# One-hots of a pair of windows written by one ScalarE instruction and moved by two SBUF DMAs

## What is computed

```python
y = affine(conv1x1(x, fc1_w, fc1_b), fc1_s, fc1_t)
nodes = windows of y, (1024, 64, 96)
idx = top_k(-dist, 9)           # nine nearest nodes of the same window
feat = concat(x_i, x_j - x_i)   # for each node i and neighbour j
h = max over j of gelu((feat @ ew + eb) * es + et)
x = affine(conv1x1(h, fc2_w, fc2_b), fc2_s, fc2_t) + x
```

## Time and profile before

| | |
|---|---|
| median of 3 runs | 4106.08 us (4105.18 to 4107.37) |
| the profiled execution's own time | 4102.94 us |
| its span | 4101.1 us |
| mean granted TensorE clock | 0.987 |
| TensorE, VectorE, ScalarE busy | 3901.0, 3821.5, 3694.2 us |
| GpSimd busy | 931.2 us |
| DMA moved | 272.31 MB, mean 66 GB/s |

### The profile page before, as it was taken

How to read it: one execution, slowest core, us unless ns; L and a number is a source line. 1 busy time by engine, 2 the same in 40 slices (tenths; PEclk the granted TensorE clock), 3 DMA queues, 4 the chain that set the end, 5 groups by cost and what they waited for, 6 DMA issues and landing times.

```text
span 4101.1 us, 79112 instructions
## 1 busy us (share of the span) xinstructions
PE 3901.0 (95%) x22752; PEld 2049.0 (50%) x22752; DVE 3821.5 (93%) x5162; ACT 3694.2 (90%) x6805; POOL 931.2 (23%) x1060
## 2 busy tenths in 40 slices
PE   4999999999999999999999999999999999999984
PEld 2445555455554555555555455555555455555542
DVE  2599999999999999999999999999999999999996
ACT  3899999999998999989999899989999899999983
POOL 0122222122222122222122222122222122222113
PEclk9999999999999999999999999999999999999996
DMA  1133342333333333343333333333333333433333
GB/s 50 24 64 76 58 88 51 67 76 66 73 73 66 60 75 73 58 80 57 69 75 66 73 61 75 62 69 76 62 79 57 70 66 67 81 61 59 62 66 65
DMA packets 100114, 272.31 MB, mean 66 GB/s; under 512 B 14946, under 2 KB 23394, under 8 KB 93476
## 3 DMA queue, kind: packets, MB, share of 16 engines
q0 software_dynamic: 65536, 184.58, 26.4%
q1 hardware_dynamic: 34116, 82.27, 7.5%
HBM read 77.68 MB, written 25.69 MB: 25 GB/s over the span
## 4 chain that ended last, share of the span: by engine, by line
PE 68%; DVE 11%; issue 9%; ACT 9%; DMA 1%; SPq 0%; POOL 0%; DVEq 0%; ACTq 0%; POOLq 0%
PE pg L648 18%; PE pmisc L576 9%; PE pg L651 8%; PE pvu L635 8%; DVE acc L1032 7%; PE pmisc L562 7%; PE pmisc L519 3%; PE pmisc L512 2%; PE pvu L621 2%; ACT MV L807 2%; PE pmisc L578 2%; DVE hid L1010 2%; PE pmisc L542 2%; PE pmisc L547 2%; ACT tapped L844 1%
## 5 line engine op out<-in xcount | busy, mean ns | idle before, releaser
L1032 DVE SCALAR_TENSOR_TENSOR acc<-hpad,w,acc 128x1024 f32<-128x1024 f32 (+1 forms) x2304 | 2618.2, 1160 | 33.5 <-issue 16.3
L648 PE MATMUL pg<-MV,VU 128*128 128x512 f32 x2048 | 1149.2, 643 | 40.7 <-ACT VU L815 29.8
L824 ACT ACTIVATE g<-pg 128x512 f32<-128x512 f32 x1536 | 912.5, 594 | 127.9 <-PE pg L651 81.4
L1010 DVE TENSOR_REDUCE hid<-g 128x192 f32<-128x1536 f32 x512 | 892.6, 1743 | 0.0
L429 POOL DMA_DIRECT2D acc<-tapped x256 | 241.3, 943 | 2106.8 <-DVE acc L1032 1818.8
L807 ACT ACTIVATE MV<-pvu,cst 64x512 f32<-64x512 f32 x1024 | 696.0, 680 | 11.8 <-PE pvu L621 5.0
L576 PE MATMUL pmisc<-acc,w 128*96 128x256 f32 x2048 | 497.1, 386 | 49.0 <-ACT acc L854 34.1
L651 PE MATMUL pg<-MV,VU 128*64 128x512 f32 x2048 | 527.5, 592 | 0.0
L562 PE MATMUL pmisc<-x,w 96*128 96x512 f32 (+1 forms) x1024 | 518.3, 608 | 7.0 <-ACT hpad L766 7.0
L635 PE MATMUL pvu<-wVU,y 97*64 97x192 f32 x4096 | 446.7, 339 | 21.8 <-ACT MV L807 21.2
L576 PEld LDWEIGHTS pmisc<-acc,w 128*96 128x96 f32 x2048 | 331.5, 165 | 262.6 <-issue 154.9
(11 more groups left out here) (101 smaller groups left out, 4447.6 us busy)
## 6 DMA issues: line engine op xcount, KB each, us to landing
acc<-tapped POOLq DMA_DIRECT2D x256, 512.0 KB, 4.9
xin<-in_x_dram SPq DMA_DIRECT2D x32, 768.0 KB, 5.8
invb<-rows_dram SPq DMA_DIRECT2D x32, 768.0 KB
x<-in_x_dram POOLq DMA_DIRECT2D x128, 192.0 KB, 4.4
res<-x POOLq DMA_DIRECT2D x128, 192.0 KB, 5.0
out_dram<-res SPq DMA_DIRECT2D x128, 192.0 KB, 3.2
hpad<-hpad SPq DMA_DIRECT2D x112, 33.0 KB, 1.8
g<-in_consts_dram SPq DMA_DIRECT2D x1, 640.0 KB
```

The costliest lines, as they stand in the source:

```text
L648: last = nc.tensor.matmul(ps[:, :], VU[:, r, part, 0:ONE128], cols[part], start=True, stop=True)
L824: nc.scalar.activation(g[:, p % 2, part, :, :], pg[(3 * p + part) % 2][:, :].rearrange("p (n k) -> p n k", k=KN), ACT.Gelu).then_inc(gelu_ ...
L1010: nc.vector.tensor_reduce(hid[:, c % 2, j, :, :], g[:, r], op=ALU.max, axis=AX.X).then_inc(hid_ready, 1)
L1032: nc.vector.scalar_tensor_tensor(out=dst, in0=src, scalar=wk, in1=dst, op0=ALU.mult, op1=ALU.add).then_inc(tap_done, 1)
```

## The change

`onehot` becomes one activation of 128 partitions into a new tile `onehots` ([128, 512] of f32, one buffer). SyncE then issues two DMAs of 64 partitions (128 KB each) that put the halves in their two places in `MV`. TensorE's `values` still waits for `onehot_ready`, now one activation; `gather` part 0 waits for a new semaphore `onehot_moved` (16 for each DMA). ScalarE's next `onehot` waits for `onehot_moved` of the pair before. The two DMAs stand at the start of SyncE's slot, ahead of its other transfers; the halo copy `UPPER_AT` moves from slot 2 to 3, the stores by one slot, the `invb` rows to the next slot. The identities in `MV` stay as they were. `hpad` loses eight unused rows, which makes room in SBUF.

```diff
-UPPER_AT, LOWER_AT = {2: FULL}, {5: FULL}
+UPPER_AT, LOWER_AT = {3: FULL}, {5: FULL}
...
-STORE_AT = {o + 2: q for o, q in W2_AT.items() if q % 2 == 1}
+STORE_AT = {o + 3: q for o, q in W2_AT.items() if q % 2 == 1}
...
+        onehots = sb("onehots", [128, KN * NODES])
...
-        hpad = sb("hpad", [128, 5, STRIP + 2, PADW])
+        hpad = sb("hpad", [128, FULL * (STRIP + 2) + STRIP // 2 + 2, PADW])
...
+            def move_onehots(P, p):
+
+                if due(count := 3 * P - 3):
+                    sp.wait_ge(gather_ready, count)
+                sp.sem_inc(sp_passed, 1)
+                if due(count := P + 1):
+                    sp.wait_ge(onehot_ready, count)
+                sp.sem_inc(sp_passed, 1)
+                for w in range(2):
+                    h = 64 * w
+                    sp.dma_start(MV[h:h + 64, p % 2, w, :], onehots[h:h + 64, :]).then_inc(onehot_moved, 16)
+
             def image(b, p0, p1):
                 for p in range(p0, p1):
+                    P = PAIRS * b + p
                     h = 1 if p < 16 else 0
                     if p % 16 == ROWS_AT and valid(b if h else b + 1, B):
-                        broadcast_norms(b, p, b if h else b + 1, h)
+                        store_norms(b, p, b if h else b + 1, h)
+                    if p % 16 == ROWS_AT + 1 and valid(b if h else b + 1, B):
+                        broadcast_norms(b if h else b + 1, h)
+                    if valid(P + 1, NPAIRS):
+                        move_onehots(P + 1, p + 1)
...
-                        if due(count := P + 1):
-                            pe.wait_ge(onehot_ready, count)
+                        if due(count := 32 * (P + 1)):
+                            pe.wait_ge(onehot_moved, count)
...
-                if due(count := 3 * P - 3):
-                    act.wait_ge(gather_ready, count)
-                for w in range(2):
-                    h = 64 * w
-                    last = nc.scalar.activation(MV[h:h + 64, p % 2, w, :].rearrange("p (n k) -> p n k", k=KN),
-                                                pone[h:h + 64, :, :].rearrange("p k n -> p n k"), ACT.Relu,
-                                                bias=nbias[h:h + 64, :], scale=1.0)
-                last.then_inc(onehot_ready, 1)
+                if due(count := 32 * P):
+                    act.wait_ge(onehot_moved, count)
+                nc.scalar.activation(onehots[:, :].rearrange("p (n k) -> p n k", k=KN), pone.rearrange("p k n -> p n k"),
+                                     ACT.Relu, bias=nbias, scale=1.0).then_inc(onehot_ready, 1)
```

More of the change, by code:

```diff
@@ L188, in sums_of, with rows_of @@
     return slice(g * STRIP * W + start, g * STRIP * W + start + n)
+def rows_of(g, first, end):
+    return slice((STRIP + 2) * g + first, (STRIP + 2) * g + end)
 def due(count):
@@ L300, in build @@
             "featT_ready", "featT_evac", "onehot_in", "onehot_ready"))
+        onehot_moved = sem("onehot_moved")
         vu_ready, vu_evac, gather_ready, gelu_done, chunk_ready = (sem(n) for n in (
@@ L338, in _, with store_norms @@
             load_half(0, 1)
-            def broadcast_norms(b, p, bi, h):
-                n = 2 * bi + h
+            def store_norms(b, p, bi, h):
                 fb, fp = when(b, p, ROWS_AT - 8)
@@ L346, in broadcast_norms @@
                 sp.dma_start(rows_dram.rearrange("k (r n) -> (k r) n", n=128), norm_rows[:, :]).then_inc(rows_stored, 16)
+            def broadcast_norms(bi, h):
+                n = 2 * bi + h
                 sp.wait_ge(rows_stored, 16 * (n + 1))
@@ L754, in shared_evac @@
                         h = 128 if gr < FULL else HALF
-                        nc.scalar.activation(hpad[0:h, gr, 1, 1:W + 1], ps[0:h, 0:W], ACT.Relu, bias=sh[0:h, :],
+                        nc.scalar.activation(hpad[0:h, (STRIP + 2) * gr + 1, 1:W + 1], ps[0:h, 0:W], ACT.Relu, bias=sh[0:h, :],
                                              scale=sc[0:h, :]).then_inc(misc_evac, 1)
@@ L764, in shared_evac @@
                         if m == 1 and t == STRIPS - 1:
-                            nc.scalar.activation(hpad[:, gr, STRIP + 1, 1:W + 1], zrow[:, :], ACT.Copy)
-                        nc.scalar.activation(hpad[:, gr, r0:r1, 1:W + 1],
+                            nc.scalar.activation(hpad[:, (STRIP + 2) * gr + STRIP + 1, 1:W + 1], zrow[:, :], ACT.Copy)
+                        nc.scalar.activation(hpad[:, rows_of(gr, r0, r1), 1:W + 1],
                                              ps[:, 0:(r1 - r0) * W].rearrange("p (row col) -> p row col", col=W),
@@ L770, in shared_evac @@
                         act.wait_ge(kept_half, 32 * s + 16)
-                        nc.scalar.activation(hpad[64:128, gr, 9, 1:W + 1], zrow[64:128, :], ACT.Copy)
+                        nc.scalar.activation(hpad[64:128, (STRIP + 2) * gr + 9, 1:W + 1], zrow[64:128, :], ACT.Copy)
                         for h, n in ((0, 8), (64, 7)):
                             last = nc.scalar.activation(
-                                hpad[h:h + 64, gr, 2:2 + n, 1:W + 1],
+                                hpad[h:h + 64, rows_of(gr, 2, 2 + n), 1:W + 1],
                                 ps[h:h + 64, 0:n * W].rearrange("p (row col) -> p row col", col=W),
@@ L837, in tap0 @@
                 nc.scalar.activation(acc[:, t % 2, sums_of(gr, 0, rows * W)].rearrange("p (row col) -> p row col", col=W),
-                                     hpad[:, gr, 0:rows, 0:W], ACT.Copy, scale=wd[:, gr, 0:1]).then_inc(tap0_done, 1)
+                                     hpad[:, rows_of(gr, 0, rows), 0:W], ACT.Copy, scale=wd[:, gr, 0:1]).then_inc(tap0_done, 1)
             def tap_product(b, p, s, gr):
@@ L926, in _ @@
             dve.sem_inc(consts_ready, 1)
-            nc.vector.memset(hpad[:, :, :, 0:1], 0.0)
-            nc.vector.memset(hpad[:, :, :, W + 1:PADW], 0.0)
+            nc.vector.memset(hpad[:, :, 0:1], 0.0)
+            nc.vector.memset(hpad[:, :, W + 1:PADW], 0.0)
             nc.vector.memset(zrow[:, :], 0.0)
@@ L1041, in image @@
                     bi = b if h else b + 1
-                    last = min(len(taps) - 1, 4) if p % PPC == 0 else 4
+                    last = max(3, min(len(taps) - 1, 4)) if p % PPC == 0 else 4
                     for a in taps[0:2]:
```

14 lines of the change are left out of this document (7 added, 7 removed).

## The result

The changed kernel took **4723.01 us** (median of 4 runs, 4714.77 to 4730.24) where the kernel before took 4106.43 in the same comparison (4105.18 to 4107.37). The ratio is 1.1502, with a 95% interval of 1.1488 to 1.1515: 617 us slower. The forecast, 4299, had the sign right and the size wrong by a factor of three, and the range ended at 4410. The profiled execution took 4720.71 us with a span of 4718.8.

What follows compares the result with a forecast made beforehand. TensorE, busy 95% of the span and holding the chain for 68%, was taken as the bound. Terms -38 + 0 + 160 + 37 + 34 = +193 us on the median 4106.1 gave 4299 us, range 4080 to 4410.

Steps and rivals of the forecast that it cites:

- ScalarE's relief, -38 us: One activation replaces two on ScalarE; 69 of TensorE's 133 waits for one-hots shorten by 0.55 us each: -38 us.
- Quiet slots, 0 us: Without GpSimd's transfers, the last half lands 2.5 us after the one-hots, inside every cover before the next gather: 0 us.
- The landing in the burst, +160 us: Slots 1, 9, 17, 25, beside GpSimd's four DMAs: landing 5.2 us against 2.73 of cover, 2.5 us on 64 slots: +160 us.
- Slots 14 and 30, +37 us: Beside one 512 KB GpSimd transfer, landing 4.1 us against 2.94 of cover, 1.2 us 32 times: +37 us.
- Behind SyncE's large transfers, +34 us: After slots 1, 9 and 25, the next one-hots queue behind 768 KB and a store: 0.7 us on 48 slots, +34 us.
- Moves cost nothing: Moving `UPPER_AT`, the stores and `invb` by a slot costs nothing, their readers being two slots or more away.
- A: Rival: transfers hidden, landing within 2.7 us also in slot 1, ScalarE's relief remains: about 4045 us; chance 0.16.
- B: Rival: partly late, landing in 3 to 4 us in busy slots, near even: about 4100 us; chance 0.13.
- D: Rival: the new activation costs as much as the two, so covers are 0.68 us shorter: 4400 us; chance 0.03.
- C: Rival: a queue that doesn't drain, the next slot also 2 us or more late: +400 us, 4500; chance 0.08.
- What would show it: Expected profile signs: ScalarE down some 350 us, gather part 0 waiting 2 to 3 us in busy slots, others unchanged.

Runs made afterwards that it cites:

- e5: Changed kernel, but one-hots of slots 1, 2, 5 and 6 of eight written straight into `MV`, the others by DMA: 4074.86 us, ratio 0.9934 to before.
- e7: Changed kernel with all one-hots written straight into `MV`, none by DMA; only the moved table rows and smaller `hpad` remain: 4080.13 us, ratio 0.9943 to before.
- E3: Changed kernel, but window 1's one-hots written straight and only window 0's sent, by one DMA of 64 partitions: 4539.93 us.
- e10: Changed kernel, but one DMA of 128 partitions takes both halves to window 0's place; window 1's gather reads a fixed table: 4625.43 us.
- e1: Changed kernel plus 22 unused matmuls ahead of gather part 0 in the slots that follow slot 1 of eight: 4457.83 us.
- e4: Changed kernel, but one-hots of slots 1, 5 and 6 of eight written straight into `MV`, the others by DMA: 4098.49 us, ratio 0.9984 to before.
- e9: Kernel before the change, with only the input half loads moved from slots 1 and 8 to 3 and 10: 4082.09 us, ratio 0.9948.
- e8: Changed kernel, but window 1's half is issued by ScalarE on its own queue: 4813.52 us.
- e6: Changed kernel, but only slots 3 and 7 of eight send one-hots by DMA, the others write them straight: 4076.32 us, ratio 0.9936 to before.
- e11: e5 with the input halves loaded in slots 3 and 10: 4077.11 us, ratio 0.9927 to before.

## Why the prediction missed

**ScalarE's relief, -38 us.** The instruction was right (0.685 us for 0.68; the one-hots' own busy time fell from 696.0 to 350.6 us, ScalarE's in all by 315 for 348). What it is worth was too high: e5 and e7 differ by 5 us. The prediction put 64 of the 133 waits in slots 1, 9, 17 and 25; the trace of before has 48 there (48.2 us), 33 in slots 3 of eight (24.3) and 29 in slots 0 (15.4). In e5 the waits of slots 0 and 3 are gone but for 5 (4.6 us), and only slot 3 is shorter, by 11 us in all: in slot 0 the landing took more than the relief gave, and part of slot 3's went the same way (31 of e5's 57 gather waits are behind slot 3, 12.4 us). A freed wait is worth what no other wait takes over.

**Quiet slots, 0 us.** The landing was right, the term wasn't quite. The second half landed 2.93 us after the one-hots, near the upper bound of 3.0: each DMA takes 2.2 to 2.3 us, and the second is issued 0.51 us behind the first, not 0.37. Slots 4, 8 and 24 kept their length. Slots 0 and 16 didn't: away from the turns both took 7.17 us and now 7.74 and 7.62. The cover there is 2.60 us, in slot 0 too, where the prediction read 3.1 or more and named slot 16 alone. That is 12 us over the 25 such slots that aren't at a turn, and it doesn't show in the table because the turns got shorter by more. E3 and e10, which land inside 2.60 us, have 7.17 in slot 16.

**The landing in the burst, +160 us.** The step "I stay under that: 5.2 us" failed. It measured 6.8 us, and the slot grew by 4.08, not 2.5: **261 us**. The working had 5.6 to 7.5 from packets and took a value below it, on the argument that the first GpSimd transfer has only just begun. The trace shows no such head start: the first packet starts 2.05 us after the issue, in a quiet slot 1.12, and then 128 packets take 3.75 us, in a quiet slot 1.32. The Trainium skill ("DMA: Bandwidth & Descriptors", Queues, rings and completion order) says that an engine drains a whole packet of descriptors of one queue before it turns to the next. The estimate of near 7 us and 270 us, which the prediction worked out from it and set aside, came out; whether by its mechanism isn't shown, since the trace doesn't tell which DMA engine moved a packet. This step was short by 101 us. By itself it would have left the forecast at 4400, still inside the range; what took the result out of the range is the next one.

**The step that isn't there: the clock.** The prediction said "a late landing stops TensorE for its full lateness" and priced nothing behind it. The stall brought the clock down to 1.2 GHz for most of the slot that followed: **314 us**, more than the stall itself, in no term and no rival. A stall of this length was in the trace of before: at the loop's turn TensorE stood still for 3.29 us and the next two matmuls took 2.08 us. The prediction has no row of it. The Trainium skill has the rule ("TensorE: Matmul & The Clock Gate", Why this matters for your kernels): idle gaps between bursts of matmuls bring the clock back to half rate. This case agrees. In the changed kernel, grouped by TensorE's stall before gather part 0, the mean granted clock of the slot behind it was 0.99 to 1.00 for stalls under 1.5 us; 0.87 for 1.5 to 2.5 us (15 slots); 0.64 for 2.5 to 3.5 (only 2 slots; in e3 46 slots, with 0.67); 0.62 for 3.5 to 4.5 (23 slots); 0.56 above (27 slots). Had the prediction's own 2.5 us been right, some of those slots would still have come behind at 0.64 to 0.87: by these rows the lost clock was worth pricing even then. That the idleness is the cause is shown by e1, where the wait is as long, TensorE is at work in it, and slot 2 takes 4.3 us less.

**Slots 14 and 30, +37 us.** About right: 4.44 us for 4.1 in slot 14. Slots 14 and 30 together cost 48 us.

**Behind SyncE's large transfers, +34 us.** Hidden in the changed kernel: slot 2 was so long that the transfers were through (2.96 us to land). It is there when slot 2 is short again, 0.6 us a slot in e1 and 0.3 in e4.

**"Moves cost nothing".** Wrong the other way: -22 us, by the turn of the loop (e7, e9; 24 us at the turns of the changed kernel).

**The rivals.** A and B fell with the landing. D fell with 0.685 us. C (a slot 2 that is late too, 4500) had the nearest number, by luck: slot 2's landing was quiet, and its loss was the clock.

**What would show it** named the right waits in the right slots, and "slots without GpSimd's transfers should be as long as before". That was false for slot 2 (and by half a microsecond for slots 0 and 16), and that one line in the new profile pointed at the missing step.

## What to carry to other kernels

A stall of a matmul engine costs its own length and then the clock of what follows: here 4 us of waiting cost 9, and 22 matmuls that compute nothing needed, 64 times, bought back 265 us. Before a transfer is put between two engines in a tight loop, ask what else the DMA engines carry at that moment; a landing of 2.9 us in quiet was 6.8 beside 1.4 MB of another queue, whichever queue issued it, and the same copies cost at most half a microsecond in slots where nothing else moved, where the landing was just longer than its cover. And when an edit also shifts a table, run the table alone.

## What I had not expected of the hardware

- In a burst the first packet of SyncE's transfer started 2.05 us after its issue in slot 1 and 2.75 in slot 6, against 1.12 in quiet. Why it starts late stays open.
- A second hardware queue gave no more of the DMA engines against GpSimd's queue (e8: 7.3 us on ScalarE's, 5.45 on SyncE's).
- At the loop's turn a 768 KB load in flight goes with 3 to 5 us more for the two slots around it. e9 shows that taking the load away from there gains them; that it slows the fetch of instructions, which has DMA queues of its own in the page (q8 and q14), is a guess that wasn't tested by itself, and e1's turns are as long without the load.

The best version measured is e5, **4074.86 us**, 0.66% under the kernel before, with e6 and e11 not told apart from it.
